# A linear-attention layer and an fp6 projection on one core: x read a second time by features, denominators inverted and spread through HBM, and attention divided after the product instead of before it

## The reference

```python
h = layernorm(x)
q, k, v = phi(h @ Wq.T + bq), phi(h @ Wk.T + bk), h @ Wv.T + bv       # per head
numerator   = q_t . cumsum_t(k v^T)            # causal, per head
denominator = max(q_t . cumsum_t(k), 1e-6)     # one number per head and token
x = x + layernorm((numerator / denominator) @ Wo.T + bo)
x = x + layernorm(mx_fp6(layernorm(x)) @ mx_fp6(Wf).T + bf)   # blocks of 32, one scale each
```

## Time and profile before

| | us |
|---|---|
| median of 3 runs | 2441.12 (2441.04 to 2442.33) |
| the profiled execution: its own time | 2443.11 |
| its span, first to last instruction | 2441.3 |
| TensorE matmuls busy | 2402.6 (98%) |
| VectorE busy | 1966.5 (81%) |
| ScalarE busy | 1168.1 (48%) |
| GpSimd busy | 1011.2 (41%) |

### The profile page before, as it was taken

One profiled execution on the slowest core, in us unless ns is written; L12 is line 12 of the kernel. 1 busy time (PEld: TensorE's weight loads), 2 busy tenths in 40 slices (PEclk: granted clock), 3 DMA queues, 4 the chain that ended last, 5 costly groups with the idle time before them and its releaser, 6 DMA issues.

```text
span 2441.3 us, 65347 instructions
## 1 busy us (share of the span) xinstructions
PE 2402.6 (98%) x27154; PEld 1972.1 (81%) x27154; DVE 1966.5 (81%) x4052; ACT 1168.1 (48%) x1965; POOL 1011.2 (41%) x1482
## 2 busy tenths in 40 slices
PE   6999999999999999999999999999999999999996
PEld 5888888888888888888888888888888888888885
DVE  7877888878888778888888887888888888878776
ACT  4544445544445444455444454444554444544442
POOL 1343344443444433444434444334444344443334
PEclk9999999999999999999999999999999999999998
DMA  4011011110111110111101111101111011111001
GB/s 159 27 46 53 28 36 53 45 53 27 36 53 53 45 53 27 36 53 45 53 28 36 53 54 45 54 27 36 53 45 53 28 36 53 53 45 53 27 19 44
DMA packets 59719, 111.36 MB, mean 46 GB/s; under 512 B 6816, under 2 KB 9248, under 8 KB 58912
## 3 DMA queue, kind: packets, MB, share of 16 engines
q1 hardware_dynamic: 59424, 107.18, 13.2%
HBM read 73.60 MB, written 33.55 MB: 44 GB/s over the span
## 4 chain that ended last, share of the span: by engine, by line
PE 97%; DVE 1%; DMA 0%; issue 0%; SPq 0%; ACT 0%; POOL 0%; POOLq 0%; DVEq 0%
PE work L354 15%; PE work L356 14%; PE work L355 14%; PE score L354 10%; PE score L356 9%; PE score L355 9%; PE work L373 8%; PE score L450 6%; PE work L485 5%; PE score L472 2%; PE state_bank L498 2%; PE work L425 1%; PE score L437 1%; DMA A<-in_wf 0%; SPq L322 0%
## 5 line engine op out<-in xcount | busy, mean ns | idle before, releaser
L997 DVE TENSOR_TENSOR A<-score,causal 128x512 f32<-128x512 f32 x512 | 317.8, 683 | 12.5 <-PE score L450 12.5
L1355 POOL TENSOR_TENSOR rs_f<-ve_f,minus_half 128x1 f32<-128x1 f32 x128 | 70.1, 547 | 598.3 <-DVE ve_f L914 598.3
L1365 POOL TENSOR_TENSOR x_res<-x_res,o_buf 128x512 f32<-128x512 f32 x128 | 179.0, 1398 | 153.3 <-ACT o_buf L626 151.9
L354 PE MATMUL work<-wv_hi,xT_hi 128*128 128x512 f32 x512 | 214.3, 419 | 1.6 <-issue 1.6
L354 PE MATMUL score<-xT_hi,wq_hi 128*128 128x512 f32 x512 | 207.1, 404 | 6.0 <-DVE KT L933 6.0
L354 PE MATMUL work<-wo_hi,oT_hi 128*128 128x512 f32 x512 | 208.1, 406 | 1.2 <-DVE oT_lo L1004 1.2
L354 PE MATMUL score<-xT_hi,wk_hi 128*128 128x512 f32 x512 | 206.3, 403 | 0.0
L356 PE MATMUL work<-wv_hi,xT_lo 128*128 128x512 f32 x512 | 201.4, 393 | 0.0
L355 PE MATMUL score<-xT_lo,wq_hi 128*128 128x512 f32 x512 | 200.8, 392 | 0.0
L356 PE MATMUL work<-wo_hi,oT_lo 128*128 128x512 f32 x512 | 200.6, 392 | 0.0
L355 PE MATMUL work<-wv_lo,xT_hi 128*128 128x512 f32 x512 | 200.6, 392 | 0.0
(11 more groups left out here) (138 smaller groups left out, 6339.0 us busy)
## 6 DMA issues: line engine op xcount, KB each, us to landing
x_in<-in_x SPq DMA_DIRECT2D x128, 256.0 KB, 4.4
x_res<-in_x SPq DMA_DIRECT2D x128, 256.0 KB, 2.9
out<-f_buf SPq DMA_DIRECT2D x96, 256.0 KB, 2.0
out<-xd SPq DMA_DIRECT2D x32, 256.0 KB, 2.1
V<-in_wk SPq DMA_DIRECT2D x4, 256.0 KB, 5.5
QT<-in_wq SPq DMA_DIRECT2D x1, 1024.0 KB, 5.9
kc<-in_wo SPq DMA_DIRECT2D x1, 1024.0 KB, 7.9
A<-in_wf SPq DMA_DIRECT2D x1, 1024.0 KB, 9.9
```

The costliest lines, as they stand in the source:

```text
L354: nc.tensor.matmul(dst, st_hi(c), mv_hi(c), start=(c == 0), stop=False)
L997: nc.vector.tensor_tensor(A[:, j, :, :], score_bank[j][:], causal[:].unsqueeze(1).to_broadcast([P, G, P]), ALU.mult).then_inc(a_set, 1)
L1355: nc.gpsimd.tensor_tensor(rs[n][:, b:b + 1], ve[n][:, b:b + 1], minus_half[:], ALU.pow).then_inc(rs_set[n], 1)
L1365: nc.gpsimd.tensor_tensor(x_res[:, b, :], x_res[:, b, :], o_buf[:, b % 2, :], ALU.add).then_inc(r_set, 1)
```

## The change

x is given to the kernel a second time, by features (`xt`, with the host's transposition of the input). The two coefficients of the first layernorm (1/sigma and shift per token) are written to HBM (`store_coef`) and read back broadcast over all partitions (`spread_coef`); POOL applies them to the feature-major x in `exp_t` (`x_scale`, two operations for each sequence), and ACT and DVE split that. `xn`, its transposes and ACT's `x_norm` are gone (tile 0 still uses them). The inverse denominators are not split: they go to HBM and come back spread over the features (`store_rden`, `spread_rden`) into `kc`. QT is not divided; DVE multiplies the result of `attend` by them on its way out of PSUM (`normalise`), and `o_hi` and `o_lo` read that SBUF result. TensorE's order and those of the other engines are written anew. The pieces of the diff below are, in this order: SP's new DMAs, TensorE's order in a turn, ACT's `x_hi`, DVE's `normalise` (`rden` is a view of `kc`, so it shows as `kc` in rows), and POOL's `x_scale`.

```diff
+            def load_xt(tile, b):
+                if b < 2:
+                    sp.wait_ge(q_set, count(tile - 1, G - 1))
+                else:
+                    sp.wait_ge(xT_set, count(tile, b - 2))
+                sp.dma_start(exp_t[:, b % 2, :], xt[b, tile].rearrange("p g t -> p (g t)")).then_inc(xt_loaded[b], 16)
+            def store_coef(tile):
+                sp.wait_ge(rstd_set["x"], count(tile, NSEQ - 1))
+                sp.dma_start(coef_dram[:], coef[:]).then_inc(coef_stored, 16)
+            def spread_rden(tile, b):
+                if b == 0:
+                    sp.wait_ge(rden_stored, 16 * (tile + 1))
+                src = rden_dram[b * DH:(b + 1) * DH, :].rearrange("(r j) t -> r (j t)", j=HPG)
+                sp.dma_start(rden[:, b, :], src.unsqueeze(1).to_broadcast([2 * G, DH // 2, HPG * P])
+                             ).then_inc(rden_loaded[b], 16)
...
                 xd_transposes(3)
                 v(0)
                 denominators()
+                past_products()
+                v(1)
+                f(3)
+                scores(0)
                 kn(0)
-                f(3)
-                spread()
-                v(1)
-                past_products()
                 v(2)
-                scores(0)
-                v(3)
-                x_transposes(0)
                 attend(0)
                 state(0)
                 scores(1)
                 kn(1)
+                v(3)
                 if cur:
                     o(i, 0)
-                x_transposes(1)
                 attend(1)
                 state(1)
                 scores(2)
                 kn(2)
                 if cur:
                     o(i, 1)
-                x_transposes(2)
                 attend(2)
...
+                    act.wait_ge(x_shifted, count(tile - 1, b))
+                    act.wait_ge(v_mm, count(tile - 1, b))
+                    nc.scalar.copy(x_cols(xT_hi, b), by_group(exp_t[:, b % 2, :])).then_inc(xT_hi_set, 1)
...
+                def normalise(b):
+                    if cur:
+                        dve.wait_ge(rden_loaded[b], 16 * (i + 1))
+                        dve.wait_ge(att_mm, count(i, b))
+                        nc.vector.tensor_tensor(rden[:, b, :], bank(("att", b))[:], rden[:, b, :], ALU.mult).then_inc(o_scaled, 1)
...
+                def x_scale(tile, b):
+                    rows = by_group(exp_t[:, b % 2, :])
+                    if b == 0:
+                        pool.wait_ge(coef_loaded, 16 * tile)
+                    pool.wait_ge(xt_loaded[b], 16 * tile)
+                    nc.gpsimd.tensor_tensor(rows, rows, by_token(0), ALU.mult).then_inc(x_scaled, 1)
+                    pool.wait_ge(x_scaled, count(tile - 1, b))
+                    nc.gpsimd.tensor_tensor(rows, rows, by_token(1), ALU.add).then_inc(x_shifted, 1)
```

More of the change, by code:

```diff
@@ L501, in state @@
                         last.then_inc(st_mm, 1)
-                def x_transposes(b):
-                    if nxt:
-                        take(pe, i, ("x", b), here, before)
-                        pe.wait_ge(xn_set, count(i + 1, b))
-                        transposes(("x", b), lambda g: xn[:, g * P:(g + 1) * P]).then_inc(x_tr, 1)
                 def o(tile, b):
@@ L686, in o_hi @@
                     if cur:
[L687 to L688 removed]
+                        act.wait_ge(o_scaled, count(i, b))
+                        nc.scalar.copy(oT_hi[:], by_group(rden[:, b, :])).then_inc(oT_hi_set, 1)
                 def past(j):
@@ L697, in seed @@
                     if cur:
-                        take(act, i, ("att", b), {0}, set())
+                        take(act, i, ("att", b), {0} if first else {-1, 0}, set())
                         if b == 0:
@@ L1273, in turn @@
                 mask(0, 3)
-                v_bias(3)
-                join(i - 1, "f", 3)
-                widen(i - 1, "f", 3)
+                f_seen(3)
+                v_bias(2)
+                normalise(0)
+                mask(1, 0)
+                o_lo(0)
                 if nxt:
                     x_lo(i + 1, 0)
-                o_lo(0)
-                if nxt:
-                    join(i + 1, "x", 3)
-                    widen(i + 1, "x", 2)
-                mask(1, 0)
                 mask(1, 1)
                 mask(1, 2)
+                if nxt:
+                    x_lo(i + 1, 1)
+                v_bias(3)
                 mask(1, 3)
```

620 lines of the change are left out of this document (318 added, 302 removed).

## The result

The changed kernel takes 2512.22 us (median, 2507.63 to 2515.01), the one before 2441.08 (2440.99 to 2442.33): the ratio is 1.0288, with a 95% interval of 1.0271 to 1.0306. I had said 2425, 0.67 for faster and 0.20 for slower. The profiled execution took 2507.63 us with a span of 2505.8.

What follows compares the result with a forecast made beforehand. TensorE was taken as the bound, never waiting in a turn. From 2443.1 us, -79.6 of its work, +61.4 of waits and +1.5 at the ends gave 2426.4, less 2.0 for the median: 2425 said, range 2385 to 2457.

Steps and rivals of the forecast that it cites:

- TensorE's loss, -79.6 us: On TensorE, dropping `x_transposes` saves 54.6 us; dropping the spread, with one change of shape fewer, saves 25.0 us.
- Waits at `o(1)` and `o(2)`, +61.4: TensorE waits 0.80 and 1.12 us a tile for the longer chain from `attend`, 61.4 us in 32 tiles.
- a rival at +0.28 for each `o_lo`: On DVE, `o_lo` with two SBUF inputs slows beside POOL by 0.28 us each: 2442 us, no change, chance 0.13.
- SP's queue holds nothing late ahead of the store: On SP, the `xt` loads ahead of the inverses' store wait only for `q_set`, long past, so nothing delays it.
- `x_scale(0)` bound by `rstd(f, 2)` at F+3.7: On POOL, `x_scale(0)` starts when `rstd(f, 2)` ends, near 3.7 us after F, the start of `f(3)`.
- `x_scale` at 1.40 us: On POOL, each of 8 new operations a turn takes 1.40 us, bounded by 1.26 and 2.10, hidden with 0.5 us slack.
- the tipping point: The length of an `x_scale` operation, 1.66 us, at which waits reach 2.49 us a tile and cancel TensorE's saving.
- The store at 2.0 us: The store of the inverse denominators to HBM lands about 2.0 us later, at F+4.4, before its spread.
- I charge nothing for the clock: TensorE's short waits ahead of `o` do not lower its granted clock, so they add 0 us for it.
- The ends, +1.5: Uncovered `o(3)` in the last tile, 0.72 us, and weight preparation in the first turn, 0.8 us, together 1.5 us.
- POOL late: `x_scale` operations longer than 1.40 us delay `x_hi(1)`, Kn(1) and `o(0)`; 2453 us at 1.75 us each, chance 0.2.
- the forecast turn (73.95 us): One steady turn: 74.57 us, less 2.54 of TensorE work, plus 1.92 of waits.

Runs made afterwards that it cites:

- e1: The changed kernel with the loads of `xt(0)` and `xt(1)` issued ahead of the coefficients' store and spread: 2462.34 us, ratio 1.0091 to the kernel before.
- e4: The changed kernel with `x_scale` reading contiguous coefficients (those of other tokens, same amount of work): 2481.79 us, ratio 1.0173 to the kernel before.
- e2: The changed kernel with the copy `kn(1)` put ahead of `x_hi(1)` on ACT: 2492.34 us, ratio 1.0211 to the kernel before.
- e18: The whole change with early `xt` loads, `normalise` writing to PSUM, and DVE, ACT and POOL reordered: 2441.07 us, ratio 0.9999 to the kernel before.
- e17: Only the x half of the change, denominators split, spread and divided as before, early `xt` loads, mended orders: 2434.27 us, 0.9969 of the kernel before.

## Why the prediction was wrong, step by step

*TensorE's loss, -79.6 us: right.* In before, all intervals of TensorE's timeline that begin or end at `x_transposes` sum to 85.2 us. In their place stand 93 direct changes of shape, 29.8 us by the earlier trace rows, and 31 steps from `kn(3)` straight to `o(2)`, 0.9 us: 54.5 against 54.6. The spread's intervals sum to 30.9, less 7.3 for products in a row, 23.6 against 22.1, and 1.5 of it is a wait in the first tile.

*Waits at `o(1)` and `o(2)`, +61.4: the mechanism right, the size short.* (1.02 - 0.03) x 32 + (1.26 - 0.03) x 32 = 71.0 us. Most tiles show what the arithmetic gave (0.85 and 1.14 start to start). Of the 9.6 us beyond it some 6 are in the ten tiles in which POOL held `o_lo(1)`, which I had as a rival at +0.28 for each `o_lo`. No `o_lo(2)` was held; at `o(2)` the rest is 2.4 us in the first tile and 0.8 in one other. Of 128 `o_lo`, 35 were held, by up to 1.4 us, 25 of them `o_lo(0)`.

*"SP's queue holds nothing late ahead of the store", and `x_scale(0)` bound by `rstd(f, 2)` at F+3.7: this is the step that failed.* In the turn shown F is 1212.44; `x_scale(0)` started at F+6.0 (5.3 on average), because the loads of `xt` stood behind a wait for the coefficients' store to land and then behind 512 KB of coefficients. I looked at what each DMA waits for, and not at what the instruction ahead of it in the queue waits for, and I gave the loads' own landing no time at all. In four turns (6, 8, 19 and 26) `xt(0)` landed by F+3.3; there `x_scale(0)` started at F+3.6, and `o(0)` did not wait. Turn 6, with F at 525.08:

```profile
528.71 1.60 POOL L1399 TENSOR_TENSOR exp_t<-exp_t,x_coef 128x512 f32<-128x512 f32 x1
...
537.74 0.39 PE L425 MATMUL work<-wv_hi,xT_lo 128*128 128x512 f32 x1
537.97 0.39 PE L423 MATMUL work<-wo_hi,oT_hi 128*128 128x512 f32 x1
```

e1 shows the price, 50 us: `o(0)`'s own wait falls by 48 and the lower clock costs 14 less, while `o(1)` and `o(2)` wait 13 more.

*`x_scale` at 1.40 us: wrong, 1.60 and 1.63 on average* (median 1.59 and 1.54), near the 1.66 at which I had put the tipping point. Four operations make 0.8 us, and with the 2.3 us of the load, less the 0.5 of slack, 2.6: `o(0)` started at F+15.3 against F+12.7. e4 prices it at 30 us while the load is late. My condition for that rival (above 1.66) was too narrow, since another cause used up the slack first.

*The store at 2.0 us: 3.9 in the median turn, 4.4 in the one shown.* The earlier trace rows has 2.0 for the stores of before; behind 1 MB of the change's own loads it is about twice that. `normalise(0)` waited for it in most tiles, but `o_lo(0)` came just in time, so it cost nothing until Kn(1) was taken off the path (e2).

*"I charge nothing for the clock": wrong at `o(0)`.* Behind the short waits of the earlier trace rows and of `o(1)` it stayed at its upper level. At 8 of the 32 `o(0)` it was at the lower one for 3.4 us (0.50 above), after TensorE had been idle for 1.8 to 2.6 us; at others, idle for up to 2.7 us, it was not, and what makes the difference is open. The trace of after has 60.3 us at the lower level against 27.6 in before, at half the rate some 16 us.

*The ends, +1.5: short in the first turn.* The first `k(0)` starts 1.5 us earlier, and the last one stands 115.2 us before the end against 114.1, but the first turn takes 83.8 us against 74.9. Of these 8.9 us, 8.4 are waits at `o(0)` to `o(2)`, which are in the sums for them.

*Not in the prediction:* the stalls inside `past_products`, nine of 0.4 to 1.8 us, 9.0 us in all.

*The sum:* 2443.1 - 79.6 + 71.0 + 52.5 (`o(0)`: 1.64 x 32) + 16 + 9.0 = 2512.0, against 2507.6 measured; the terms overlap a little in the clock's. So of the 87 us by which I missed, about 70 are `o(0)` with its clock, 10 the longer waits at `o(1)` and `o(2)` (6 of them by `o_lo`'s lock) and 9 the stalls.

The rival on the other side, "POOL late", had the right place and the end of the right chain, at a fifth of the chance. But it rested on the length of `x_scale` alone and, at the 1.60 and 1.63 us measured, would not have forecast a slower kernel; the late load was in no rival. e18 comes near the forecast turn (73.95 us), with a median of 74.1 and a mean of 74.25, by an early load, an `o_lo` that reads PSUM and another order. What was wrong was that the change as made reaches it.

## What to carry to other kernels

Where queues are in order, ask of each moved instruction not what it waits for but what everything ahead of it waits for, on SP above all: a load that could go at once stood behind another DMA's landing and its 512 KB successor, and two moved lines were worth 50 us. A change that takes 80 us from the bound engine and adds a link to a chain moves waits about; only a version in which each of them has been looked up in the trace and mended (e18, e17) says what the change is worth, and here the whole was worth nothing and half of it 0.3%. Look at the first turn by itself, too: in e17 and e18 it took back some 8 us of what the other turns gained. When engines are near their full load in one stage, moving a step ahead makes another late: predict the one behind it before counting a gain.
